# Angle and norm products of the second layer's attention: nine matmuls over 64 output rows written as nine over all 128

## The reference

```python
q = (hidden_states @ Wq.T + bq)   # 16 heads of 16
k = (hidden_states @ Wk.T + bk)   # 8 heads of 16
q = q * cos + _rotate_half(q) * sin
k = k * cos + _rotate_half(k) * sin
def _softmax_kernel(x, R):        # R: 8 x 16
    n = jnp.sqrt(jnp.sum(x * x, axis=-1, keepdims=True))
    x = x / jnp.maximum(n, 1e-06)
    p = jnp.einsum('...d,ed->...e', x, R)
    feats = jnp.concatenate([jnp.sin(p), jnp.cos(p)], axis=-1)
    return feats / math.sqrt(F)
kv = jnp.einsum('bhsf,bhsd->bsfd', kp, v)
out = jnp.einsum('bhsf,bsfd->bhsd', qp, kv)
```

## Time and profile before

| | us |
|---|---|
| three runs: median (lowest to highest) | 595.71 (595.42 to 597.21) |
| the profiled execution | 597.21 |
| its span, first to last instruction | 595.4 |
| PE busy (matmul) | 522.0, 88% of the span |
| DVE busy | 334.4, 56% |
| ACT busy | 312.5, 52% |
| POOL busy | 328.9, 55% |

### The profile page before, as it was taken

How to read it: one execution, slowest core, us unless ns; L and a number is a source line. 1 busy time by engine, 2 the same in 40 slices (tenths; PEclk the granted TensorE clock), 3 DMA queues, 4 the chain that set the end, 5 groups by cost and what they waited for, 6 DMA issues and landing times.

```text
span 595.4 us, 9656 instructions
## 1 busy us (share of the span) xinstructions
PE 522.0 (88%) x2951; PEld 397.9 (67%) x2951; DVE 334.4 (56%) x884; ACT 312.5 (52%) x739; POOL 328.9 (55%) x235
## 2 busy tenths in 40 slices
PE   0998988799777899999999999999988898899981
PEld 0655776588566678778787777988856444465561
DVE  3389832314056282652935629343356898999643
ACT  1215126365464776757757577575632238666530
POOL 3000438868677586685866858854312024888860
PEclk9999999899797999999999999999999999999997
DMA  9940629887886986675675756866368102556667
GB/s 289 375 149 6 165 66 216 183 173 187 209 240 155 251 215 150 128 169 112 145 175 127 169 117 142 187 147 142 35 171 264 52 21 78 81 88 98 97 80 220
DMA packets 87281, 90.39 MB, mean 152 GB/s; under 512 B 26688, under 2 KB 75264, under 8 KB 86848
## 3 DMA queue, kind: packets, MB, share of 16 engines
q1 hardware_dynamic: 66608, 61.50, 36.1%
q0 software_dynamic: 19584, 27.24, 27.5%
q10 hardware_dynamic: 1040, 1.05, 0.5%
HBM read 65.32 MB, written 22.60 MB: 148 GB/s over the span
## 4 chain that ended last, share of the span: by engine, by line
PE 40%; DVE 18%; issue 15%; DMA 9%; ACT 9%; POOL 8%; SPq 0%; POOLq 0%; ACTq 0%; DVEq 0%
PE bank L559 8%; DMA expert_sums<-expert_weights,token_of_slot 7%; PE bank L896 6%; PE bank L904 3%; PE bank L905 3%; PE bank L551 2%; PE bank L523 2%; POOL tiles L1098 2%; PE bank L1804 2%; DVE sum_squares L686 2%; ACT normed L607 2%; POOL expert_sums L866 2%; POOL expert_weights L858 2%; POOL expert_sums L1105 2%; PE bank L491 2%
## 5 line engine op out<-in xcount | busy, mean ns | idle before, releaser
L866 POOL DMA_INDIRECT expert_sums<-expert_weights,token_of_slot x79 | 131.1, 1659 | 57.1 <-ACT expert_weights L928 39.4
L858 POOL DMA_INDIRECT expert_weights<-normed_x,token_of_slot x79 | 92.2, 1167 | 111.5 <-DVE token_of_slot L366 47.2
L896 PE MATMUL bank<-expert_weights 128*88 128x128 f32 x632 | 84.2, 276 | 1.3 <-ACT expert_weights L921 1.2
L896 PEld LDWEIGHTS bank<-expert_weights 128*88 128x88 f32 x632 | 74.6, 159 | 2.1 <-issue 2.1
L559 PE MATMUL bank<-out_weights,expert_weights 128*128 128x256 f32 x256 | 60.1, 380 | 1.4 <-ACT expert_weights L644 1.4
L928 ACT ACTIVATE expert_weights<-bank,chosen_bf 128x256 f32<-128x256 f32 x79 | 37.7, 478 | 36.4 <-issue 22.2
L904 PE MATMUL bank<-expert_weights 88*128 88x256 f32 x158 | 48.4, 388 | 6.9 <-ACT expert_weights L928 5.7
L1105 POOL DMA_INDIRECT expert_sums<-expert_weights,token_of_slot x23 | 46.3, 2011 | 14.5 <-issue 5.5
L559 PEld LDWEIGHTS bank<-out_weights,expert_weights 128*128 128x128 f32 x256 | 46.4, 190 | 8.2 <-ACT expert_weights L644 3.1
L719 DVE SCALAR_TENSOR_TENSOR expert_weights<-bank,blocks_valid 128x64 f32<-128x64 f32 x32 | 7.1, 221 | 75.6 <-ACT expert_weights L621 68.7
L905 PE MATMUL bank<-expert_weights 89*128 89x256 f32 x158 | 48.1, 385 | 0.0
(11 more groups left out here) (272 smaller groups left out, 1084.7 us busy)
## 6 DMA issues: line engine op xcount, KB each, us to landing
expert_weights<-experts_out SPq DMA_DIRECT2D x79, 192.8 KB
expert_weights<-experts_in SPq DMA_DIRECT2D x79, 176.0 KB
expert_weights<-L_ffn_wi SPq DMA_DIRECT2D x32, 128.0 KB
expert_weights<-w_comp SPq DMA_DIRECT2D x1, 2048.0 KB, 9.2
expert_weights<-fold_g SPq DMA_DIRECT2D x1, 2048.0 KB, 13.4
expert_sums<-zeros SPq DMA_DIRECT2D x2, 1024.0 KB, 17.9
expert_weights<-L_ffn_wo SPq DMA_DIRECT2D x16, 128.0 KB
normed<-expert_sums SPq DMA_DIRECT2D x2, 1024.0 KB, 5.6
```

What stands on the lines that cost most here:

```text
L858: nc.gpsimd.indirect_dma_start(xt0[g % 4], None, xn0, bass.IndirectOffsetOnAxis(ap=MAP[:, g:g + 1], axis=0)).then_inc(gathered[g % 4], 16)
L866: nc.gpsimd.indirect_dma_start(sums0[g % 2], bass.IndirectOffsetOnAxis(ap=MAP[:, g:g + 1], axis=0), yt0[g % 2], None, compute_op=ALU.add). ...
L896: ins = nc.tensor.matmul(ps[5][0:DHB, c * P:(c + 1) * P], w[:, k * DH + c * DHB:k * DH + (c + 1) * DHB], xT0[g % NXT][:, k * P:(k + 1) * P ...
```

## The change

All nine products of a call now write all 128 rows of their bank. For bank 7, the weights of block 0 are the window [matrix | zeros] of RCOS or RSIN and those of block 1 the window [zeros | matrix]; the four products accumulate into the whole bank, where before each half of the rows had a pair of its own. For bank 1, block 2 uses the window [matrix | zeros] and then the three products with BONES, whose windows are 128 columns wide and so start 64 columns further left, add to the same rows. The accumulation starts once a bank, and ends once. The order changes too: cosine and sine of a block now follow one another, and both products of block 2 stand ahead of the three with BONES instead of between them.

```diff
@@ def angles(pe, hf)
             block = lambda room, c: room[hf][:, c * HALF:(c + 1) * HALF]
-            rcos, rsin = RCOS[:, HR1:2 * HR1], RSIN[:, HR1:2 * HR1]
-            for w, room in ((rcos, QCOS), (rsin, QSIN)):
-                for c in range(2):
-                    ins = nc.tensor.matmul(ps[7][c * HR1:(c + 1) * HR1, :], w, block(room, c), start=(w is rcos), stop=(w is rsin))
+            wide = lambda w, c: w[:, (1 - c % 2) * HR1:(1 - c % 2) * HR1 + P]
+            for c in range(2):
+                nc.tensor.matmul(ps[7][:, :], wide(RCOS, c), block(QCOS, c), start=(c == 0), stop=False)
+                ins = nc.tensor.matmul(ps[7][:, :], wide(RSIN, c), block(QSIN, c), start=False, stop=(c == 1))
             ins.then_inc(ang_ps, 1)
+            nc.tensor.matmul(ps[1][:, :], wide(RCOS, 2), block(QCOS, 2), start=True, stop=False)
+            nc.tensor.matmul(ps[1][:, :], wide(RSIN, 2), block(QSIN, 2), start=False, stop=False)
             for c in range(NQK):
-                if c < 2:
-                    nc.tensor.matmul(ps[1][0:HR1, :], (rcos, rsin)[c], block((QCOS, QSIN)[c], 2), start=(c == 0), stop=(c == 1))
-                lo = HR1 + (NQK - 1 - c) * P // D1
-                ins = nc.tensor.matmul(ps[1][HR1:, :], BONES[:, lo:lo + HR1], block(QSQ, c), start=(c == 0), stop=(c == NQK - 1))
+                lo = (NQK - 1 - c) * P // D1
+                ins = nc.tensor.matmul(ps[1][:, :], BONES[:, lo:lo + P], block(QSQ, c), start=False, stop=(c == NQK - 1))
             ins.then_inc(ang_ps, 1)
```

## The result

The changed kernel is slower: 602.55 us, the median of four executions (600.21 to 604.28), against 595.57 us of the kernel before. The ratio is 1.0128, with a 95% interval of 1.0091 to 1.0165. Carried over to the 595.71 us from which I had forecast, that is 603.3 us, with an interval of 601.1 to 605.5; the forecast was 601.4, within 599.7 to 603.1. So the way was right, the size was not quite: 603.3 lies 0.2 us above the range; 5.7 us were forecast, and this timing says 7.6, with 5.4 to 9.8 as its bounds. The two sides of the ratio are of very different weight: 34 executions of the changed kernel, the four above among them, have a mean of 603.51 us, and 603.51 over 595.89, the mean of only four executions of the kernel before, is 1.0128.

A forecast was written before the change was run, and what follows sets the result against it. PE's second angles call was taken as fully on the path, the first beside DVE's routing with 0.57 us slack. First call 2.4 plus second 3.3 gave +5.7 on 595.71: 601.4 us, range 599.7 to 603.1.

The forecast's parts named there:

- the range: Whole kernel: 599.7 to 603.1 us, from the second call's start, the borders, (d) and 1.8 us between runs.
- Price of a call: PE, each angles call: nine unpaired products, two records each, 0.43 us a record, 7.74 us.
- Rival (a): PE, angles: pairing only in the records, 128-row products keep the old pace; 595.4 us, chance 4%.
- The borders: PE, between 128 and 64 columns of weights around angles: 0.09 + 0.09 + 0.10 us go away.
- Loads of 128 columns: PE, angles: weight loads of 0.19 us expected hidden, at L991's pace of 0.43 us a record.
- Rival (c): PE, angles: 128-column loads don't hide, 36 records by 0.19 us, 6.8 us on top; 608.2 us, chance 2%.
- First call: PE, angles(pe, 0): 3.11 us later, less the idle 0.57 before the second call; 2.4 us taken.
- Rival (b): First call of angles: surplus stays hidden, only the second call's 3.3 us counts; 599.0 us, chance 4%.
- Sum at the first expert tile: First expert tile's transposes (L1127) on PE: 2.4 + 3.3 us later, +5.7 us, starting at 495.9.
- Carried to the end: Expert stage after L1127: the 5.7 us shift passes through ACT, DVE, POOL and DMA to the end undiminished.
- (d): Expert stage: POOL slips against DVE by a tile, plus or minus 0.9 to 1.9 us; inside the 89% main case.
- none of two successive ones can lie beside the other: PE, angles: with all nine products writing 128 rows, the pairing (0.86 us a pair) goes.

The follow-up runs named there:

- e3_first: Kernel before, with only the first call of angles writing 128 rows and the second keeping its pairs; ratio 1.0049 (1.0015 to 1.0084).
- e4_order64: Kernel before, with the changed kernel's product order but still 64 output rows; ratio 1.0028 (1.0001 to 1.0055).
- e9_blocks: Kernel before at 64 rows, reordered: all four lower-half products first, then the five for the upper half; only execution 597.72 us.

## Why the prediction was right in its steps and short in its range

- **Price of a call.** Right: 7.73 us for 7.74, 18 records 0.43 apart, no pairs. Rival (a), that the pairs are only how records look, falls.
- **The borders.** Right, and small: 0.09 + 0.09 + 0.10 us went. The drain on changing the tiling mode that the Trainium skill's page "TensorEngine Tiling (Array Packing)", section "Tiling Modes", names would fit these 0.09 us, though no run shows that the borders are a drain; the lost pairs outweigh them.
- **Loads of 128 columns.** Rival (c) falls: the weight loads of 0.19 us are hidden, as the 0.86 us of a product shows.
- **First call.** Right: 3.11 forecast and 3.09 measured (from the first of the eight L991 to L1034 it was 480.69 - 470.80 = 9.89 us, and is 479.75 - 466.77 = 12.98), less the 0.57 idle us, forecast as 2.4; e3_first shows 2.44. Rival (b) falls. DVE wasn't late; it is DVE that now waits 2.08 us for the slot map.
- **Sum at the first expert tile.** Right: 5.7 forecast, 5.63 or 5.64 in all five traces of the changed kernel.
- **Carried to the end.** Right: 16.2 us from L1127 to the first scatter-add (508.05 - 491.85), 16.11 before, and the rest of the span the same within its own scatter, which was (d).
- **What failed** is the last term, the range, and the base under it. I took the scatter between executions from three of them, 1.8 us (595.42 to 597.21), added 5.7 to their median and set the upper edge 1.7 above the sum. The runs showed a standard deviation of about 2 us and single times of the unchanged kernel from 592.88 to 601.61 us, and later means of it from 596.26 to 598.09, above the 595.71 of the three. The measured 7.6 us sets 34 executions of the changed kernel against four such low ones. So 5.64 us of it is the change as the traces show it, and the other 2 go, as far as is known, with that base: against 28, 24 and 15 executions of the kernel before, the later sets give +6.0, +4.9 and +6.2. That the ratios of all five timings of the changed kernel lie between 1.0110 and 1.0128, above 1.0095, is left open; no trace shows a place for more, but the traces are mostly of quick executions.
- I had written that "none of two successive ones can lie beside the other" as if pairs needed neighbours. For the sum it made no difference, since nothing is left to pair with among 128-row products; e4_order64 shows that the reason given was too narrow.

## What to carry to other kernels

Float32 products with 64 output rows that go to different halves of the rows ran two at a time here, so widening each to 128 rows with zeros doubles the time of every pair (a call went from 4.45 to 7.73 us, one of its nine having had no partner), though the number of instructions stays the same. Whether this matters is decided by who releases the call: subtract the engine's idle time ahead of it (0.57 us here) from the surplus, and count the rest in full if the chain of waits passes through. And for a change of 1%, compare a stretch between two instructions in the traces, which here repeated within 0.02 us, before trusting a base of four executions that scatter by 2 us.

## What the runs showed of the hardware that I had not expected

PE didn't start products strictly in program order where they write different halves of the rows. In e4_order64 a product for the upper rows started together with the one for the lower rows that stood two places ahead of it, past a third (L1020 at 473.10 beside L1017 at 473.09, ahead of the sine of block 2); in e9_blocks one that stood four, then three behind waited 1.77 us (472.97 to 474.74) although its half of the rows had nothing to do. The Trainium skill, page "TensorE: Matmul & The Clock Gate", section "Part 3: Packing small matmuls — row/col tiling", says that matmuls start and end in strict program order; the starts at 471.32 to 473.10 of e4_order64 differ, and this text goes by the measurement. The ends are modelled in the profile, so no run here speaks on them.
